# Block 0 scored by f32 matmuls from raw operands, ks_t bounded and split during block 0, and a scale of its own for each block of x

## The reference

```python
scores = jnp.einsum('nd,md->nm', x, ks)
scores = jax.nn.leaky_relu(scores, negative_slope=0.2)
scores = jnp.where(adj > 0, scores, -9e15)
attn = jax.nn.softmax(scores, axis=1)
y = x + jnp.einsum('nm,md->nd', attn, ks)
out = (y - mean(y)) / sqrt(var(y) + 1e-5)      # over each row of 128
```

## Time and profile before

| | |
|---|---|
| median of 3 runs | 1696.18 us (1684.28 to 1696.39) |
| the profiled execution | 1695.82 us, its span 1694.0 us |
| busy: PE, DVE, POOL, ACT | 1624.7, 1344.3, 1240.6, 1143.1 us |
| granted PE clock, mean | 0.996 |
| read from HBM, written | 289.41 MB, 4.19 MB |

### The profile page before, as it was taken

How to read it: one execution, slowest core, us unless ns; L and a number is a source line. 1 busy time by engine, 2 the same in 40 slices (tenths; PEclk the granted TensorE clock), 3 DMA queues, 4 the chain that set the end, 5 groups by cost and what they waited for, 6 DMA issues and landing times.

```text
span 1694.0 us, 34690 instructions
## 1 busy us (share of the span) xinstructions
PE 1624.7 (96%) x14528; PEld 1540.4 (91%) x14528; DVE 1344.3 (79%) x1311; ACT 1143.1 (67%) x1297; POOL 1240.6 (73%) x650
## 2 busy tenths in 40 slices
PE   2679999999999999999999999999999999999997
PEld 1479999999999999999999999999999999999996
DVE  7988888878888888888888878887878787878860
ACT  4456767777666777766676766767676777676664
POOL 0176778787778787777877777878777878777887
PEclk9999999999999999999999999999999999999999
DMA  9734445445544554554455444445544544554410
GB/s 365 271 149 180 159 179 184 172 171 182 171 173 176 181 181 167 180 180 167 171 184 183 166 175 181 170 172 183 184 159 178 184 175 172 177 178 171 173 56 7
DMA packets 69660, 295.84 MB, mean 175 GB/s; under 512 B 6016, under 2 KB 34688, under 8 KB 36736
## 3 DMA queue, kind: packets, MB, share of 16 engines
q1 hardware_dynamic: 69504, 293.63, 49.0%
HBM read 289.41 MB, written 4.19 MB: 173 GB/s over the span
## 4 chain that ended last, share of the span: by engine, by line
POOL 64%; issue 33%; DMA 1%; DVE 1%; POOLq 0%; ACT 0%; SPq 0%; PE 0%; ACTq 0%; DVEq 0%
POOL ring L236 62%; POOL rstd L249 1%; DMA ring<-in_x_t 1%; POOLq L233 0%; POOL var L246 0%; POOL neg_mean L241 0%; DVE kt_lo L367 0%; SPq L169 0%; POOL shift L251 0%; SPq L172 0%; ACT kt_hi L274 0%; PE weighted L519 0%; ACT normed L322 0%; DVE ring L406 0%; DVE running L416 0%
## 5 line engine op out<-in xcount | busy, mean ns | idle before, releaser
L236 POOL TENSOR_TENSOR ring<-ring,floor 128x1024 f32<-128x1024 f32 x512 | 1200.4, 2384 | 218.8 <-ACT floor L308 218.6
L519 PE MATMUL weighted<-k_rows,ring 128*128 128x129 f32 x8192 | 999.1, 275 | 3.8 <-ACT ring L303 3.8
L519 PEld LDWEIGHTS weighted<-k_rows,ring 128*128 128x128 f32 x8192 | 955.1, 192 | 11.2 <-ACT ring L303 5.9
L298 ACT ACTIVATE scores<-scores,shrink 128x1024 f32<-128x1024 f32 x512 | 555.6, 1085 | 466.9 <-PE scores L487 466.9
L406 DVE SCALAR_TENSOR_TENSOR ring<-adj_sb,scores 128x1024 f32<-128x1024 int32 x512 | 624.4, 1220 | 287.9 <-ACT scores L298 285.3
L485 PE MATMUL scores<-xt_hi,kt_hi 128*128 128x256 f16 x2048 | 560.5, 274 | 54.2 <-DVE xt_lo L373 29.5
L419 DVE TENSOR_TENSOR running<-ring,running 128x1024 f32<-128x1024 f32 x480 | 586.5, 1222 | 0.1
L486 PE MATMUL scores<-xt_lo,kt_hi 128*128 128x256 f16 x2048 | 560.4, 274 | 0.0
L487 PE MATMUL scores<-xt_hi,kt_lo 128*128 128x256 f16 x2048 | 560.2, 274 | 0.0
L303 ACT ACTIVATE ring<-ring 128x1024 f32<-128x1024 f32 x512 | 535.8, 1047 | 16.2 <-POOL ring L236 16.2
L485 PEld LDWEIGHTS scores<-xt_hi,kt_hi 128*128 128x128 f16 x2048 | 201.6, 98 | 77.5 <-DVE ring L406 29.9
(11 more groups left out here) (34 smaller groups left out, 171.6 us busy)
## 6 DMA issues: line engine op xcount, KB each, us to landing
adj_sb<-in_adj SPq DMA_DIRECT2D x256, 1024.0 KB, 4.8
ring<-in_ks_t SPq DMA_DIRECT2D x8, 512.0 KB, 6.5
ring<-in_x_t SPq DMA_DIRECT2D x8, 512.0 KB, 12.8
xt_raw<-in_x_t SPq DMA_DIRECT2D x32, 128.0 KB, 4.8
k_rows<-in_ks SPq DMA_DIRECT2D x8, 512.0 KB, 7.4
x_row<-in_x SPq DMA_DIRECT2D x32, 128.0 KB, 4.8
out<-normed SPq DMA_DIRECT2D x32, 128.0 KB, 5.1
```

The lines of the kernel that those rows point to most:

```text
L236: nc.gpsimd.tensor_tensor(here, here, below, ALU.subtract).then_inc(gap_ready, 1)
L298: nc.scalar.activation(here, here, ACT.Prelu, scale=shrink[:, :], alpha=SLOPE).then_inc(bent_ready, 1)
L519: last = nc.tensor.matmul(weighted[:, b % 2, j * LANES:(j + 1) * LANES], ring[:, g % RING, t, j * P:(j + 1) * P], k_rows[:, rows, 0:LANES] ...
```

## The change: what it does

The prologue goes. Block 0 is scored from raw operands: ks_t is loaded, chunk by chunk of 1024 keys, into the place of the key rows (`k_rows`), and each of the four key tiles takes one f32 matmul of 256 columns instead of three f16 ones. ks_t is bounded by ACT in slots 0 to 8, split by ACT into kt_hi in slots 10 to 17, and kt_lo is made by POOL for chunks 0 to 5 (a multiplication in place and a subtraction, before POOL's first gap) and by DVE for chunks 6 and 7, in slots 23 and 25. The rows of ks are loaded over the raw ks_t afterwards, chunk c in slot 14 + 2c. x_t is no longer loaded whole: each block b from 1 on has its own scale. DVE takes the block's magnitude in slot 16b - 11, POOL spreads it in slot 16b - 10, DVE makes the scale in slot 16b - 9 and the factor for `bend` in slot 16b - 8 (for block 1 in slots 9 and 10).

```diff
+    AT_BOUND, AT_HIGH = (0, 1, 3, 3, 5, 6, 8, 8), 10
+    POOL_LOWS = 6
+    AT_LOW = {23: 6, 25: 7}
...
             load_xt(0)
-            for n in range(ADJS):
-                load_adj(n)
+            load_ks_t(0)
+            load_adj(0)
+            load_ks_t(1)
+            load_adj(1)
+            load_ks_t(2)
+            load_ks_t(3)
+            load_adj(2)
+            load_ks_t(4)
+            load_ks_t(5)
+            load_adj(3)
+            load_ks_t(6)
+            load_ks_t(7)
             load_xt(1)
...
+                if 14 <= s < 14 + 2 * STEPS and s % 2 == 0:
+                    load_rows(s // 2 - 7)
...
+            def spread_mag_x(b):
+                pool.wait_ge(mag_x_ready, b)
+                wait(pool, scale_x_step, SCALE_STEPS * (b - 1))
+                nc.gpsimd.partition_all_reduce(mag_all[:, 0:1], mag[:, 0:1], P, bass.bass_isa.ReduceOp.max)\
+                    .then_inc(mag_x_all_ready, 1)
+
+            def low_ks_t(c):
+                tiles, cols = chunk(c)
+                here = k_rows[:, tiles, 0:D]
+                high = kt_hi[:, cols].rearrange("p (t m) -> p t m", m=P)
+                pool.wait_ge(kt_hi_ready, c + 1)
+                pool.wait_ge(scores_ready, (c + 1) * GROUPS // STEPS)
+                nc.gpsimd.tensor_scalar(here, here, scale_k, 1.0, ALU.mult, ALU.mult).then_inc(kt_scaled_ready, 1)
+                pool.wait_ge(kt_scaled_ready, c + 1)
+                nc.gpsimd.tensor_tensor(kt_lo[:, cols].rearrange("p (t m) -> p t m", m=P), here, high, ALU.subtract)\
+                    .then_inc(kt_lo_ready, 1)
...
+            spread_mag_k()
+            spread_mag_x(1)
+            for c in range(POOL_LOWS):
+                low_ks_t(c)
             for s in SLOTS:
+                b = whole(s, -10)
+                if b is not None and b > 1:
+                    spread_mag_x(b)
...
+                for c in range(STEPS):
+                    if s == AT_BOUND[c]:
+                        bound_ks_t(c)
+                    if s == AT_HIGH + c:
+                        high_ks_t(c)
...
+                if s == AT_BOUND[-1]:
+                    magnitude_k()
+                if s == AT_BOUND[-1] + 1:
+                    magnitude_x(1)
+                    power(1, mag_k_all_ready, scale_k_step, 0)
+                if s == AT_BOUND[-1] + 2:
+                    power(0, mag_x_all_ready, scale_x_step, 0)
+                    make_shrink(1)
+                if s in AT_LOW:
+                    low_ks_t(AT_LOW[s])
+                b = whole(s, -11)
+                if b is not None and b > 1:
+                    magnitude_x(b)
+                b = whole(s, -9)
+                if b is not None and b > 1:
+                    power(0, mag_x_all_ready, scale_x_step, b - 1)
+                b = whole(s, -8)
+                if b is not None and b > 1:
+                    make_shrink(b)
...
+                if b == 0:
+                    pe.wait_ge(ks_t_loaded[c], 16)
+                    if j == 0:
+                        pe.wait_ge(xt_loaded[0], 16)
+                    for t in range(QUAD):
+                        last = nc.tensor.matmul(scores[:, g % 2, t, :], k_rows[:, j * QUAD + t, 0:D], xt_raw[:, 0, :],
+                                                start=True, stop=True)
+                    last.then_inc(scores_ready, 1)
+                    return
                 if j == 0:
-                    pe.wait_ge(xt_lo_ready, b + 1)
-                if b == 0:
-                    pe.wait_ge(kt_lo_ready, j * QUAD * P // STEP + 1)
+                    pe.wait_ge(xt_lo_ready, b)
+                if b == 1:
+                    wait_low(pe, c)
```

More of the change, by code:

```diff
@@ L163, in whole, with chunk, wait_low, load_ks_t @@
             return b if over == 0 and 0 <= b < BLOCKS else None
+        def chunk(c):
+            return slice(c * TILES // STEPS, (c + 1) * TILES // STEPS), slice(c * STEP, (c + 1) * STEP)
+        def wait_low(eng, c):
+            if c < POOL_LOWS:
+                eng.wait_ge(kt_lo_ready, c + 1)
+            else:
+                eng.wait_ge(kt_lo_late, c + 1 - POOL_LOWS)
         @block.sync
         def _(sp):
[L167 to L172, removed]
+            def load_ks_t(c):
+                tiles, cols = chunk(c)
+                sp.dma_start(k_rows[:, tiles, 0:D], ks_t[:, cols].rearrange("d (t m) -> d t m", m=P))\
+                    .then_inc(ks_t_loaded[c], 16)
+            def load_rows(c):
+                tiles, _ = chunk(c)
+                wait_low(sp, c)
+                sp.dma_start(k_rows[:, tiles, 0:D], ks[:, tiles, :]).then_inc(k_rows_loaded[c], 16)
             def load_adj(n):
@@ L297, in bend @@
                 here = scores[:, g % 2, :, :]
-                nc.scalar.activation(here, here, ACT.Prelu, scale=shrink[:, :], alpha=SLOPE).then_inc(bent_ready, 1)
+                b = g // GROUPS
+                if b > 0 and g % GROUPS == 0:
+                    act.wait_ge(shrink_ready, b)
+                nc.scalar.activation(here, here, ACT.Prelu, scale=shrink[:, b % 2:b % 2 + 1] if b else 2.0 ** -SHRINK,
+                                     alpha=SLOPE).then_inc(bent_ready, 1)
             def exponentials(g):
@@ L351, in power @@
+            def power(column, ready, step, n):
                 one = slice(column, column + 1)
[L352 removed]
+                done = SCALE_STEPS * n
+                dve.wait_ge(ready, n + 1)
                 nc.vector.tensor_scalar(expo[:, one], mag_all[:, one].bitcast(I32), EXP_MASK, None, ALU.bitwise_and)\
[L354 to L355 removed]
+                    .then_inc(step, 1)
+                dve.wait_ge(step, done + 1)
@@ L447, in finish @@
                                                    accum_out=y_sum[:, j:j + 1]).then_inc(y_ready, 1)
-            for c in range(EARLY, STEPS):
-                split_ks_t(c)
             for s in SLOTS:
```

141 lines of the change are left out of this document (60 added, 81 removed).

## The result

The changed kernel takes **1891.6 us** (median of 4 runs, 1888.2 to 1893.8) against 1695.6 us for the kernel before: ratio 1.117 with an interval of 1.114 to 1.120. It is 11.7% slower. The prediction was 1855 us and a range of 1670 to 1990, with 0.79 on slower: sign, mechanism and place came out as written; the forecast is 36 us short.

What follows compares the result with a forecast made beforehand. PE was taken to bound from slot 22 on. 1694.0 - 19 (prologue and fill) + 154 (configuration changes) + 25 (clock) + 0 (first burst) = 1854, plus 1.8 outside the span: 1855 us, range 1670 to 1990.

Steps and rivals of the forecast that it cites:

- What bounds, and where: From slot 22 on PE bounds; work off PE costs nothing there unless it makes PE wait.
- 2L - 7.7: PE's lateness in us per steady block, L being one configuration change; hidden up to L = 3.85, 5.3 us at 6.5.
- The price of a change of configuration: POOL, between third and fourth gap, blocks 2 to 31: 6.5 us each way, middle of 0 to 13.1; +154 us in all.
- 1830: The sum in us, instead of 1855, if the skill page's about 6 us for a first call held.
- The clock: Half clock on PE after waiting for the fourth weigh: 0 to 49 us over 29 blocks, half taken, +25.
- Lateness at the whole clock: PE's score after the fourth gap comes 5.3 us late in each of 29 blocks, +154 us.
- Prologue and fill: Start up to slot 18: first mask at 9.7, mask(18) at 60.1 instead of 79.6; gain 19 us, 16 to 22.
- The first burst: Block 0's gaps on POOL: a stall of 10.1 us replaces the old 10.3; 0, -10 to +8.
- What was covered: DVE's additions, its scale in slot 16b - 9, SP's key-row waits and f32 scores in the fill cost nothing more.
- Cheap changes: Rival: a configuration change on POOL takes under 3.85 us, giving 1668 or 1689 us; chance 0.20.
- a kt_lo that waits out the burst: Within the cheap-changes rival: DVE's kt_lo in slot 23 waits until POOL's first burst ends, giving 1689 us.
- Changes of 9 us and more: Rival: a configuration change on POOL takes 9 to 13 us, giving 2026 us and more; chance 0.14.

Runs made afterwards that it cites:

- hold_weigh: The changed kernel plus 32 f16 matmuls of 254 columns that nobody reads, in front of each block's fourth weigh: 1849.4 us.
- switch_only: one_scale plus two changes of POOL's configuration, nothing between them, in front of the fourth gap of blocks 2 to 31: 1885.8 us.
- one_scale: The changed kernel with block 1's scale used for all later blocks, so no magnitude, all-reduce or scale from block 2 on: 1666.2 us.
- pe_spread: The changed kernel with POOL's all-reduce from block 2 on replaced by one f32 matmul with the unit matrix and a maximum on DVE: 1673.9 us.
- delay_long: one_scale plus 19 powers of 2 columns on POOL in front of the fourth gap of blocks 2 to 31, no configuration change: 1872.2 us.
- before_dose: The kernel before plus one all-reduce that nobody reads, in front of the fourth gap of blocks 2 to 31: 1918.8 us.
- delay_short: one_scale plus 10 powers of 2 columns on POOL in front of the fourth gap of blocks 2 to 31: ratio 0.995.
- twice: The changed kernel with a second all-reduce, read by nobody, directly ahead of the first between the same two configuration changes: 1913.2 us.

## Why the prediction was right, and where it was short

**What bounds, and where.** Right. PE bounds, a delay on POOL between gap 3 and gap 4 costs nothing up to a threshold, and what is beyond it is lost: 6.56 us cost nothing, 12.41 and 13.4 cost 5.9 and 7.25 a block, the clock's part included. The walk back from the score at 312.77 to gap 4, which gave 2L - 7.7, is borne out by hold_weigh: with the 6.0 and 7.2 us measured it gives 5.5, against 5.69.

**The price of a change of configuration.** Right in the mean: 6.0 and 7.0 against 6.5. It was the middle of 0 and 13.1, with no row near it; that it hit is luck as much as reading. The first pair of the earlier trace rows, which cost nothing, did not stand for the later ones; why it was free, no run tested. The page of the Trainium skill named there (GPSIMD Engine Reference, 2.1 Instruction dispatch) has about 6 us for the first call to newly loaded code. The traces agree with the size, and with its warning that no instruction shows it; they show more than a first call: it is paid in both directions in every block from 2 to 31, and in switch_only without any call in between. Its 6 us in both directions would be 12, where 13.0 were measured. With 12, the prediction's own 29 x (2L - 7.7) gives 125 and a sum of 1826; the 1830 that stands there is 4 off.

**The clock: the step that was short.** I took half of 1.7 us, 0.85 a block, +25 us. It is 1.56 a block, 45 us: 20 of the 36 us missing. The 3.17 us idle from which I took it was followed by half clock for 3.4 us; behind the 4.34 us of the steady block (3.4 were forecast) it lasts twice as long, some 6.8. That 45 lies near the upper end of 49 is chance. The upper end was all the work that 3.4 us at half clock take, 1.7 us. In the changed kernel PE is busy 53.2 us in the mean of the 29 blocks for 50.4 us of work, so the half clock takes 2.8, and nearly half of that is hidden: at the whole clock, in hold_weigh, the next two scores wait for their masks instead (0.18 and 0.17 us behind the fourth weigh at 370.29).

**Lateness at the whole clock.** 5.3 forecast, 5.69 measured: 11 us.

**Prologue and fill.** Forecast 19 at slot 18, measured 20.7: first mask 10.24 for 9.7, slot 18 at 58.94 for 60.1.

**The first burst.** Forecast 0, measured a loss of 5.3 (20.7 gained at slot 18, 15.4 left at the second block). The two changes are longer there than later, 7.96 and 7.48 us, so the fourth gap ended at 88.0 and not at 86.2, and the half clock behind the stall (0.88 over the stretch from 62.79 to 120.81) was not in the sum. 20 + 11 - 1.7 + 5.3 is 35, and the median is 0.9 us above the profiled execution: these are the 36.

**What was covered.** Right: DVE's additions, the scale in slot 16b - 9, SP's loads and the f32 scores. One_scale leaves them out or keeps them, pe_spread has all of them, and the two differ by the matmul's 0.22 us a block alone.

**The rivals.** Cheap changes (0.20) would have given 1668 to 1689; one_scale, which is what that case describes, measured 1666. Its second half, a kt_lo that waits out the burst, is seen in delay_long. Changes of 9 us and more: none, the longest was 8.0, and 8.94 in before_dose.

## What to carry to other kernels

An operation of GpSimd that needs another configuration is not priced by its record (0.38 us here) but by two changes around it, 13 us of the engine in this kernel. Its place decides what that costs: 2.9 us a block ahead of the burst that feeds PE, 7.25 inside it. So look first for the same result from an engine that need not change, here one matmul with the unit matrix at 0.22 us. And when a wait of PE is forecast, price the clock behind it with the wait: here 1.56 us for 4.3 of idle.

## What the runs showed of the hardware that was not expected

- A change of configuration in the midst of POOL's work costs 6.0 us one way and 7.0 the other, in each of 29 blocks, 8.0 and 7.5 the first time; its own records say 6 to 83 ns.
- A DVE instruction that reads two tensors of SBUF can wait far longer than one instruction of POOL: 23.20 us beside a burst of gaps in delay_long and 14.30 in before_dose, in others of these kernels 1.3 to 2.9 for the same kt_lo. Several kernels have two levels of time: 1672 and 1695 in delay_short, 1902 and 1924 in twice, 1910 and 1928 in before_dose. The kernel before has them too: three of its 38 executions on record take 1684 to 1686 us and all others 1695 to 1697, 10 us apart, the size of its stall in the earlier trace rows. That this wait makes the levels is likely and not shown, since no kernel was profiled at both.
- In the changed kernel the clock fell behind PE's wait in all 29 blocks, for about 3.4 or about 6.8 us at its lower level (clock 0.97 or 0.94 over the block); delay_long, whose blocks all wait 3.4 us, has the two in turn.
- A column of 128 numbers out to DRAM took SP 9.1 us of waiting in the mean, beside loads of adj.
